# P normalised before it is split, and P times V in four column tiles, for 30 of the 64 attention groups

## The chip, the cores and the metric

One Trainium2 chip, one of its cores. The metric is the device time of the whole kernel in microseconds (us); the time of an execution is that from launch to end on this core.

## What is computed

A cross-attention layer and a gated feed-forward layer, each with a residual, on 16 sequences of 128 tokens and 1024 features.

```python
query, key, value = norm(x) @ w_q.T, ctx @ w_k.T, ctx @ w_v.T      # 32 heads of 32, 8 groups of keys and values
scores    = einsum('bghnd,bgsd->bghns', query, key) / 32 ** 0.5
scores    = where(mask, scores, finfo.min)
attention = softmax(scores)
out       = einsum('bghns,bgsd->bghnd', attention, value)          # P times V
x = x + out @ w_out.T
x12 = norm(x) @ w12.T + b12; x1, x2 = split(x12)
x = x + (silu(x1) * x2) @ w3.T + b3
```

## The kernel before

The tokens are worked through in 8 blocks of two sequences (`U = 2`). A block has 8 groups; group g holds four heads of both sequences, thus 8 score tiles of 128x128. There are 64 groups, and the main loop `for t in range(1, NB + 1): for s in range(STEPS)` runs one step for each: step g = 8(t-1)+s does the scores of group g, and beside them the projections of block t and the output projection of block t-2. The feed-forward layer follows the loop; its first 512 tokens begin in the loop's last block.

Each engine has its own queue, written out by hand in the same order of steps, and no engine changes the order of its queue.

- TensorE in step g: `scores(g)` (8 matmuls, L1406), the step's first unit (`product`, L1349: a projection, or a quarter of an output projection), `turn_attn(g-3)` (two transposes, L1366), the second unit, `weigh(g-2)` (24 matmuls, L1424 to L1428). The last step of a block has the two V projections as its units, four half tiles of the rows of x to transpose (`turn_x`, L1358) around `turn_attn`, and a small transpose and product (`turn_top` L1335, `spread_top` L1342).
- `weigh(g)`: P transposed (128 x 128, two fp16 pieces, high and low) is the stationary operand, V (32 columns and a column of ones) streams. Three products for each of 8 heads; the column of ones gives the row sum of P. The result goes to `B_AV`. VectorE divides it by the row sums (`divide`, L1836 and L1838), TensorE turns it, and ScalarE and VectorE split it into two fp16 pieces (`attn_hi` L1125, `attn_lo` L1844) for the output projection.
- ScalarE in step g: `exps(g, 0)` (four heads, L1153, in place in `e`), the first unit's high piece, `attn_hi(g-3)`, `exps(g, 1)`, the second unit's high piece, `prob_hi(g)` (the high piece of P, L1160), and in steps 4 and 6 `scale_rows` (L1236). In the last step of a block its queue is `exps`, the V projection's high piece (`v_hi`, L1144), two of `x_hi` (L1118), `attn_hi`, `exps`, two of `x_hi`, `v_hi`, `prob_hi`.
- VectorE in step g: `divide(g-3)`, `mask_scores(g)` (8 instructions, L1820), low pieces of the units (L1790), `attn_lo(g-3)`, and maxima, row statistics and residuals as they fall. Up to group 11 it also makes the low piece of P (L1830).
- GpSimd (POOL) in step g: `prob_lo(g-1)` (two instructions, L936) from group 12 on; in the first two steps of a block `split_ctx` (four pieces of three instructions each, L870 to L874); in steps 2 and 3 a `root` (L884, a power of minus one half on one column, and L891).
- The queue of SyncE issues all DMAs, among them `turn_prob(g)` (L699, a transposing DMA of P from `p_split` to `prob_t`) in step g+1, after it has waited for the low piece of P and for `weigh(g-2)`.

`e`, `p_split` and `prob_t` have two buffers each, used by group parity. The results of TensorE's units, transposes of x and turned attention outputs rotate through five PSUM banks (`begin`): a unit waits until VectorE has read what stood in its bank. By that rotation, in the last step of a block the second half of the second x tile takes the bank of the first V projection, and the second V projection that of the first x half.

## Time and profile before

| | us |
|---|---|
| median of 3 runs | 1043.22 |
| lowest, highest | 1041.37, 1044.38 |
| span of the profiled execution, first to last instruction | 1040.4 |
| TensorE busy in it | 1017.7 (98%) |
| VectorE, ScalarE, POOL busy in it | 661.6, 447.3, 498.6 |

The span leaves out what lies around the instructions: 2.8 us against the median. In the views, PE is TensorE's matmuls, PEld its weight loads, DVE is VectorE, ACT ScalarE, POOL GpSimd, SPq the queue of SyncE. A matmul's duration counts its way through the array, so consecutive matmuls overlap in the listing, and what one costs is read from start to start. In a timeline a row can hold several instructions (x24) of one line.

### The profile page before, as it was taken

What the parts mean: (1) busy time and instruction counts of PE and PEld (TensorE: products, weight loads), DVE (VectorE), ACT (ScalarE), POOL (GpSimd) and SP (SyncE); (2) the same over time, 40 slices, a digit from 0 to 9 for tenths busy, and PEclk for the clock granted to TensorE, in tenths of its full rate; (3) what the DMA queues carried; (4) which work ended last, traced back from release to release, by engine and by line L of the source; (5) the groups of instructions that cost most, each with busy time, mean ns of one, the idle gap of its engine ahead of it and who ended that gap; (6) DMA issues with size and microseconds to landing.
All of it is one profiled execution on the core that took longest, in us unless ns stands there. A gap on an engine that the chain in (4) does not pass through costs nothing.

```text
span 1040.4 us, 21876 instructions
## 1 busy us (share of the span) xinstructions
PE 1017.7 (98%) x8400; PEld 695.6 (67%) x8400; DVE 661.6 (64%) x2080; ACT 447.3 (43%) x983; POOL 498.6 (48%) x476
## 2 busy tenths in 40 slices
PE   7897999999999999999999999999999999999998
PEld 6786868869687696886655544444444888468853
DVE  6789977767787777888646234636864447625431
ACT  6768556557465574664766210123431112202100
POOL 2869923727337273379958596158742301212000
PEclk9999999999999999999999999999999999999999
DMA  9669686998989999789946715494758631974201
GB/s 367 227 160 197 168 216 168 222 247 222 248 211 229 230 245 244 179 236 232 268 94 123 253 71 203 94 345 160 272 200 185 235 112 40 236 230 122 83 31 51
DMA packets 230776, 199.12 MB, mean 191 GB/s; under 512 B 177040, under 2 KB 187280, under 8 KB 225808
## 3 DMA queue, kind: packets, MB, share of 16 engines
q1 hardware_dynamic: 230672, 197.72, 69.0%
q8 instruction: 67, 1.10, 0.4%
q14 instruction: 37, 0.30, 0.1%
HBM read 119.04 MB, written 35.65 MB: 149 GB/s over the span
## 4 chain that ended last, share of the span: by engine, by line
PE 87%; DVE 6%; DMA 1%; ACT 1%; issue 0%; SPq 0%; DVEq 0%
PE bank_dense L1349 52%; PE bank_spare L1349 13%; PE bank_score L1494 6%; PE bank_spare L1494 6%; PE bank_av L1494 3%; PE bank_score L1406 2%; DVE arena_attn L1820 2%; DVE arena_attn L1830 1%; PE bank_av L1424 1%; PE bank_av L1428 1%; PE bank_av L1426 1%; PE bank_dense L1366 1%; DMA k_scratch<-arena_in 1%; PE bank_spare L1358 0%; PE bank_dense L1358 0%
## 5 line engine op out<-in xcount | busy, mean ns | idle before, releaser
L1153 ACT ACTIVATE arena_attn<-arena_attn,arena_in 128x128 f32<-128x128 f32 x512 | 162.7, 391 | 94.6 <-DVE arena_in L1820 93.6
L1349 PE MATMUL bank_dense<-arena_rows,arena_in 128*128 128x256 f16 (+1 forms) x1272 | 175.2, 295 | 1.9 <-POOL arena_in L874 1.0
L936 POOL TENSOR_TENSOR arena_attn<-arena_attn 128x512 f16<-128x512 f32 x89 | 102.6, 1170 | 148.8 <-ACT arena_attn L1160 148.8
L1349 PE MATMUL bank_dense<-arena_attn,arena_rows 128*128 128x512 f16 x768 | 166.4, 379 | 0.0
L1349 PEld LDWEIGHTS bank_dense<-arena_rows,arena_in 128*128 128x128 f16 x1272 | 123.0, 98 | 43.1 <-DVE arena_in L1668 1.6
L1820 DVE CUSTOM_DVE_ANT_0 arena_attn<-bank_score,arena_in 128x128 f32<-128x128 f32 x512 | 143.5, 346 | 0.4 <-PE bank_score L1406 0.4
L1349 PEld LDWEIGHTS bank_dense<-arena_attn,arena_rows 128*128 128x128 f16 x768 | 75.2, 98 | 90.2
L1349 PE MATMUL bank_dense<-arena_out,arena_attn 128*128 128x512 f16 x576 | 127.8, 379 | 0.0
L1349 PEld LDWEIGHTS bank_dense<-arena_out,arena_attn 128*128 128x128 f16 x576 | 55.5, 98 | 63.3
L1349 PE MATMUL bank_spare<-arena_rows,arena_in 128*128 128x256 f16 (+1 forms) x648 | 87.6, 292 | 0.0
L1349 PE MATMUL bank_dense<-arena_out,arena_in 128*128 128x512 f16 x384 | 83.0, 379 | 0.0
L874 POOL TENSOR_TENSOR arena_in<-arena_in 128x512 f16<-128x512 f32 x62 | 74.2, 1196 | 5.0
L1349 PEld LDWEIGHTS bank_spare<-arena_rows,arena_in 128*128 128x128 f16 x648 | 63.0, 98 | 19.0
L1907 DVE SCALAR_TENSOR_TENSOR arena_out<-bank_dense,small,arena_out 128x256 f32<-128x256 f32 x64 | 28.0, 478 | 75.0 <-PE bank_dense L1349 75.0
L884 POOL TENSOR_TENSOR small<-small 128x1 f32<-128x1 f32 x32 | 19.9, 622 | 107.2 <-DVE small L1709 107.2
L1349 PEld LDWEIGHTS bank_dense<-arena_out,arena_in 128*128 128x128 f16 x384 | 37.6, 98 | 45.3
L1160 ACT ACTIVATE arena_attn<-arena_attn 128x1024 f16<-128x1024 f32 x64 | 67.2, 1050 | 1.0 <-DMA arena_attn<-arena_attn 0.7
L1349 PE MATMUL bank_dense<-arena_in 128*128 128x256 f16 x456 | 52.8, 273 | 1.4 <-DVE arena_in L1675 1.4
L1424 PE MATMUL bank_av<-v_high,arena_attn 128*128 128x33 f16 x512 | 45.5, 178 | 6.7 <-DMA arena_attn<-arena_attn 6.7
L1003 POOL TENSOR_TENSOR arena_out<-arena_out,arena_rows 128x1024 f32<-128x1024 f32 x12 | 29.2, 2462 | 47.1 <-DMA arena_out<-x_scratch 47.1
L1859 DVE SCALAR_TENSOR_TENSOR arena_rows<-bank_dense,small,arena_rows 128x256 f32<-128x256 f32 x48 | 21.0, 479 | 46.9 <-PE bank_dense L1349 43.9
L1349 PEld LDWEIGHTS bank_dense<-arena_in 128*128 128x128 f16 x456 | 43.8, 98 | 7.8 <-DVE arena_in L1675 1.7
(219 smaller groups left out, 1890.8 us busy)
## 6 DMA issues: line engine op xcount, KB each, us to landing
arena_rows<-x SPq DMA_DIRECT2D x32, 512.0 KB, 6.1
arena_in<-w_scratch SPq DMA_DIRECT2D x64, 256.0 KB, 3.1
arena_attn<-q_scratch SPq DMA_DIRECT2D x48, 256.0 KB, 4.5
arena_rows<-w_t SPq DMA_DIRECT2D x12, 1024.0 KB, 6.2
arena_rows<-ctx_t SPq DMA_DIRECT2D x8, 1024.0 KB, 6.1
q_scratch<-arena_attn SPq DMA_DIRECT2D x16, 512.0 KB, 5.1
x_scratch<-arena_rows SPq DMA_DIRECT2D x16, 512.0 KB, 3.8
arena_out<-x_scratch SPq DMA_DIRECT2D x16, 512.0 KB, 5.9
```

What stands on the lines that cost most here:

```text
L874: pool.tensor_tensor(lo, buf, hi, ALU.subtract).then_inc(ready, 1)
L936: ins = pool.tensor_tensor(p_split[:, g % 2, u, 1], e[:, g % 2, u], p_split[:, g % 2, u, 0], ALU.subtract)
L1003: ins = pool.tensor_tensor(y_res[:, u], y_res[:, u], b3_all, ALU.add)
L1153: ins = act.activation(head, head, ACT.Exp, bias=neg_max[:, g % 2, h:h + 1], scale=-1.0)
L1160: act.activation(p_split[:, g % 2, :, 0], e[:, g % 2], ACT.Copy).then_inc(s_phi, 1)
L1349: ins = pe.matmul(dst, lhs(a, c), rhs(b, c), start=(c == chunks[0] and n == 0), stop=(c == chunks[-1] and n == 2))
L1406: ins = pe.matmul(B_SCORE[:, HALF * u + SEQ * j:HALF * u + SEQ * j + SEQ], q_stack[0:3 * DH, m // 4, j, m % 4, SEQ * u:SEQ * u + SEQ], k_s ...
L1424: pe.matmul(B_AV[:, at:at + VW], prob_t[:, g % 2, u, 0, j], v_high[:, a % 2, u, m], start=True, stop=False)
L1494: ins = pe.matmul(seven(v, j), weights[:, a, P * c:P * c + P], rows[:, b, c], start=(c == 0 and n == 0), stop=(c == 3 and n == 2))
L1820: ins = dve.tensor_tensor_reduce(out=e[:, g % 2, h // HPG, SEQ * (h % HPG):SEQ * (h % HPG) + SEQ], in0=B_SCORE[:, SEQ * h:SEQ * h + SEQ], ...
L1859: ins = dve.scalar_tensor_tensor(out=cols, in0=bank("o", b, q)[:, 256 * n:256 * n + 256], scalar=c_out[:, 2 * h + n:2 * h + n + 1], in1=co ...
L1907: ins = dve.scalar_tensor_tensor(out=cols, in0=bank("y", f, q)[:, 256 * k:256 * k + 256], scalar=c_ffn[:, 2 * h + k:2 * h + k + 1], in1=co ...
```

## The change

For the groups of `NORMED` (from 8 to 47, those with g mod 8 of 2 or more: 30 groups, six in each of five blocks):

- `exps` has each Exp also sum its row (`accum_out`, into `p_sum`).
- GpSimd, in step g behind `prob_lo(g-1)`, runs `norm_prob(g)`: for each half, when its `exps` are done, `p_sum` times 2^-14, to the power -1 (both on 128x4), and P times that (128x512, in place in `e`). `by_vector` holds for no group, so VectorE's `norm_prob` is never called.
- `prob_hi(g)` waits for that instead of for `exps`. The rest of the split of P is as before.
- `weigh(g)` has V's 32 columns as the stationary operand and P transposed (128 columns) as the moving one, 24 matmuls, those of head j in column tile j (`tile_position=(0, 32 j)`). The result is the turned output, written into a rotating bank. There is no `divide` and no `turn_attn`.
- `weigh(g)` stands where `turn_attn(g)` stood, in the middle of step g+3, no longer at the end of step g+2.
- `attn_hi` and `attn_lo` take off the 2^14.
- waits on `s_av` and `s_avread` count only the divided groups, or are for the `a` result (`weighed`).

```diff
+NORMED = [g for g in range(8, 48) if g % 8 >= 2]
+P_SCALE = 2.0 ** 14
...
+        def weighed(g):
+
+            return (s_dense, done("a", g)) if g in NORMED else (s_av, divided_count(g))
...
                 if g >= 2:
-                    sp.wait_ge(s_av, g - 1)
+                    sp.wait_ge(*weighed(g - 2))
                 sp.dma_start_transpose(prob_t[:, g % 2].rearrange("p u s j n -> p (u s j) n"),
...
+            def norm_prob(g):
+                n = normed_count(g - 1, by_pool)
+                for u in range(U):
+                    pool.wait_ge(s_exp, 2 * g + u + 1)
+                    pool.tensor_scalar(inv_pool[:, u], p_sum[:, g % 2, u], 1 / P_SCALE, None, ALU.mult).then_inc(s_pinv, 1)
+                    pool.wait_ge(s_pinv, 2 * (U * n + u) + 1)
+                    pool.tensor_tensor(inv_pool[:, u], inv_pool[:, u], minus_one.broadcast_to([P, HPG]), ALU.pow)\
+                        .then_inc(s_pinv, 1)
+                    pool.wait_ge(s_pinv, 2 * (U * n + u) + 2)
+                    heads = e[:, g % 2, u].rearrange("p (j n) -> p j n", j=HPG)
+                    ins = pool.tensor_tensor(heads, heads, inv_pool[:, u].rearrange("p (j o) -> p j o", o=1)
+                                             .broadcast_to([P, HPG, SEQ]), ALU.mult)
+                ins.then_inc(s_pnorm, 1)
...
                     if GROUPS * (t - 1) + s > PLO_ALONE:
                         prob_lo(GROUPS * (t - 1) + s - 1)
+                    if by_pool(GROUPS * (t - 1) + s):
+                        norm_prob(GROUPS * (t - 1) + s)
                     if t < NB and s in (0, 1):
                         split_ctx(t, halves[s])
...
-                    ins = act.activation(head, head, ACT.Exp, bias=neg_max[:, g % 2, h:h + 1], scale=-1.0)
+                    if g in NORMED:
+                        ins = act.activation(head, head, ACT.Exp, bias=neg_max[:, g % 2, h:h + 1], scale=-1.0,
+                                             accum_out=p_sum[:, g % 2, u, j:j + 1])
...
             def prob_hi(g):
-                act.wait_ge(s_exp, 2 * g + 2)
+                if by_pool(g):
+                    act.wait_ge(s_pnorm, normed_count(g, by_pool))
...
+                if g in NORMED:
+                    dst = begin("a", g)
+                    terms_of_out = ((v_high, 0), (v_low, 0), (v_high, 1))
+                    for u in range(U):
+                        for n, (v, piece) in enumerate(terms_of_out):
+                            for j in range(HPG):
+                                ins = pe.matmul(dst[DH * j:DH * j + DH, SEQ * u:SEQ * u + SEQ],
+                                                v[:, a % 2, u, m, 0:DH], prob_t[:, g % 2, u, piece, j],
+                                                start=n == 0, stop=n == 2, tile_position=(0, DH * j))
+                    ins.then_inc(s_dense, 1)
+                    return
...
-                    if g >= 3:
+                    if g >= 3 and g - 3 in NORMED:
+                        weigh(g - 3)
+                    elif g >= 3:
                         turn_attn(g - 3)
...
-                    if g >= 2:
+                    if g >= 2 and g - 2 not in NORMED:
                         weigh(g - 2)
...
             def divide(g):
+                if g in NORMED:
+                    return
```

## Rows read from the trace of the kernel before

**Rows 1.** The page: busy time of each engine; the chain that ended last, by engine.

```profile
PE 1017.7 (98%) x8400; PEld 695.6 (67%) x8400; DVE 661.6 (64%) x2080; ACT 447.3 (43%) x983; POOL 498.6 (48%) x476
...
PE 87%; DVE 6%; DMA 1%; ACT 1%; issue 0%; SPq 0%; DVEq 0%
```

**Rows 2.** Window, us: length, busy (instructions) of PE, PEld, DVE, ACT, POOL; clock, DMA.

```profile
135.00:200.00 65.00, 65.00 (x678) 50.06 (x677) 47.46 (x205) 38.33 (x98) 28.22 (x32) 1.00 0.80 199
```

**Rows 3.** Timeline of PE (start, duration, engine, line), end of one step.

```profile
211.78 0.38 PE L1366 MATMUL bank_dense<-arena_in 128*128 128x128 f32 x2
211.99 2.78 PE L1349 MATMUL bank_dense<-arena_in 128*128 128x256 f16 x24
214.61 0.18 PE L1424 MATMUL bank_av<-v_high,arena_attn 128*128 128x33 f16 x1
...
215.22 0.61 PE L1406 MATMUL bank_score<-arena_attn 96*128 96x128 f16 x8
215.66 0.60 PE L1349 MATMUL bank_dense<-arena_out,arena_attn 128*128 128x512 f16 x2
```

**Rows 4.** Timeline of PE, last step of a block, and the same of the block before.

```profile
168.69 0.61 PE L1406 MATMUL bank_score<-arena_attn 96*128 96x128 f16 x8
...
233.35 0.61 PE L1406 MATMUL bank_score<-arena_attn 96*128 96x128 f16 x8
233.79 0.27 PE L1335 MATMUL bank_spare<-arena_in 128*1 128x128 f32 x1
233.91 2.78 PE L1349 MATMUL bank_spare<-arena_in 128*128 128x256 f16 x24
...
237.62 1.04 PE L1358 MATMUL bank_spare<-arena_in,arena_rows 128*128 128x128 f32 x8
238.54 0.28 PE L1349 MATMUL bank_dense<-arena_in 128*128 128x256 f16 x1
```

**Rows 5.** Timeline of ACT, step of group 22 and its successor, the last of its block.

```profile
230.33 0.38 ACT L1125 ACTIVATE arena_attn<-bank_dense 128x256 f16<-128x256 f32 x1 [2.52 <-PE bank_dense L1366]
230.61 1.26 ACT L1153 ACTIVATE arena_attn<-arena_attn,arena_in 128x128 f32<-128x128 f32 x4
...
233.23 1.05 ACT L1160 ACTIVATE arena_attn<-arena_attn 128x1024 f16<-128x1024 f32 x1
234.18 1.23 ACT L1236 ACTIVATE arena_rows<-arena_rows,arena_in,small 128x1024 f32<-128x1024 f32 x1
235.53 1.28 ACT L1153 ACTIVATE arena_attn<-arena_attn,arena_in 128x128 f32<-128x128 f32 x4
236.78 0.39 ACT L1144 ACTIVATE v_high<-bank_spare 128x256 f16<-128x256 f32 x1
```

**Rows 6.** Timeline of DVE in the same step.

```profile
237.42 0.41 DVE L1790 SCALAR_TENSOR_TENSOR v_low<-bank_spare,v_high 128x256 f16<-128x256 f32 x1
```

**Rows 7.** Timeline of POOL: a root, prob_lo, and the start of the context's split.

```profile
135.21 0.55 POOL L884 TENSOR_TENSOR small<-small 128x1 f32<-128x1 f32 x1 [4.50 <-DVE small L1709]
135.84 0.19 POOL L891 TENSOR_TENSOR arena_in<-arena_in,small 128x1 f32<-128x1 f32 x1
...
178.12 2.28 POOL L936 TENSOR_TENSOR arena_attn<-arena_attn 128x512 f16<-128x512 f32 x2 [6.15 <-ACT arena_attn L1160]
180.35 1.04 POOL L870 TENSOR_TENSOR arena_in<-arena_rows,small 128x512 f32<-128x512 f32 x1
181.46 0.61 POOL L872 CAST arena_in<-arena_in 128x512 f16<-128x512 f32 x1
...
186.30 2.28 POOL L936 TENSOR_TENSOR arena_attn<-arena_attn 128x512 f16<-128x512 f32 x2
```

**Rows 8.** Timeline of ACT at the start: the read of a row sum and the next activation.

```profile
10.65 0.19 ACT L1031 ACTIVATION_READ_ACCUMULATOR arena_in<-arena_attn 128x1 f32 x1
10.75 1.04 ACT L1031 ACTIVATE arena_in<-arena_attn 128x1024 bf16<-128x1024 f32 x1
```

**Rows 9.** DMA issues: kind, count, median us to landing; transposes of P.

```profile
arena_attn<-arena_attn SPq DMA_TRANSPOSE x64, 4.9
```

More of the change, by code:

```diff
@@ L302, in later_unit, with by_vector, by_pool, normed_count @@
     return UNITS * (f - PLAIN) + i
+def by_vector(g):
+    return g in NORMED and g % GROUPS < 2
+def by_pool(g):
+    return g in NORMED and g % GROUPS >= 2
+def normed_count(g, kind=lambda n: n in NORMED):
+    return sum(kind(n) for n in range(g + 1))
+def divided_count(g):
+    return g + 1 - normed_count(g)
 def plo_count(g):
@@ L409, in xattn_ffn @@
         kept, with_6, with_5, with_7 = [terms[:, 0], terms[:, 1]], terms[:, 2], terms[:, 3], terms[:, 4]
+        p_sum = part(arena_attn, 59, 1, F32)[:, 0:2 * U * HPG].rearrange("p (r u j) -> p r u j", r=2, u=U)
+        inv_pool = part(arena_attn, 60, 1, F32)[:, 0:U * HPG].rearrange("p (u j) -> p u j", u=U)
+        minus_one = part(arena_attn, 62, 1, F32)[:, 0:1]
+        inv_vector = part(arena_attn, 61, 1, F32)[:, 0:U * HPG].rearrange("p (u j) -> p u j", u=U)
         k_stack = part(arena_attn, 63, 4).rearrange("p (b g n) -> p b g n", b=2, g=4)
@@ L1124, in attn_hi @@
                     act.wait_ge(s_dense, done("o", (g - RING) // GROUPS, 3))
-                act.activation(attn_t[:, g % RING, 0], bank("a", g)[:, 0:AB], ACT.Copy).then_inc(s_dhi, 1)
+                act.activation(attn_t[:, g % RING, 0], bank("a", g)[:, 0:AB], ACT.Copy,
+                               scale=1 / P_SCALE if g in NORMED else 1.0).then_inc(s_dhi, 1)
             def q_hi(t, m):
@@ L1362, in turn_attn @@
             def turn_attn(g):
-                pe.wait_ge(s_avread, g + 1)
+                pe.wait_ge(s_avread, divided_count(g))
                 dst = begin("a", g)
@@ L1831, in prob_lo, with norm_prob @@
                    .then_inc(s_plo, 1)
+            def norm_prob(g):
+                n = normed_count(g - 1, by_vector)
+                for u in range(U):
+                    dve.wait_ge(s_exp, 2 * g + u + 1)
+                    dve.reciprocal(inv_vector[:, u], p_sum[:, g % 2, u]).then_inc(s_vinv, 1)
+                    dve.wait_ge(s_vinv, U * n + u + 1)
+                    heads = e[:, g % 2, u].rearrange("p (j n) -> p j n", j=HPG)
+                    ins = dve.scalar_tensor_tensor(out=heads, in0=heads, scalar=P_SCALE,
+                                                   in1=inv_vector[:, u].rearrange("p (j o) -> p j o", o=1)
+                                                   .broadcast_to([P, HPG, SEQ]), op0=ALU.mult, op1=ALU.mult)
+                ins.then_inc(s_vnorm, 1)
             def divide(g):
+                if g in NORMED:
+                    return
                 av = B_AV[:, 0:VW * U * HPG].rearrange("p (h w) -> p h w", w=VW)
-                dve.wait_ge(s_av, g + 1)
+                dve.wait_ge(s_av, divided_count(g))
                 dve.reciprocal(inv_sum[:, :].rearrange("p (h o) -> p h o", o=1), av[:, :, DH:DH + 1]).then_inc(s_inv, 1)
-                dve.wait_ge(s_inv, g + 1)
+                dve.wait_ge(s_inv, divided_count(g))
                 dve.tensor_tensor(attn.rearrange("p (h w) -> p h w", w=DH), av[:, :, 0:DH],
@@ L1843, in attn_lo @@
                 dve.wait_ge(s_dhi, hi_count("a", g))
+                if g in NORMED:
+                    dve.scalar_tensor_tensor(out=attn_t[:, g % RING, 1], in0=bank("a", g)[:, 0:AB], scalar=1 / P_SCALE,
+                                             in1=attn_t[:, g % RING, 0], op0=ALU.mult, op1=ALU.subtract).then_inc(s_dread, 1)
+                    return
                 dve.tensor_tensor(attn_t[:, g % RING, 1], bank("a", g)[:, 0:AB], attn_t[:, g % RING, 0], ALU.subtract)\
@@ L2007, in _ @@
                         attn_lo(g - 3)
+                    if by_vector(g):
+                        norm_prob(g)
                     if t < NB - 1 and s == 5:
```

23 lines of the change are left out of this document (17 added, 6 removed).

## The prediction

> **What bounds the kernel now.** I read the page first: TensorE is busy for 98% of the span and carries 87% of the chain that ended last; no other engine is above 64% [rows 1]. A busy share alone doesn't say that TensorE sets the pace, so I took windows over the main loop: from 135 to 200 us TensorE is busy for all 65.00 us at full clock, VectorE for 47.46, ScalarE for 38.33 and GpSimd for 28.22 [rows 2]. All of the changed groups but the first few run in such windows, from about 125 to 460 us. So a microsecond taken from TensorE there is a microsecond of the kernel, as long as the other queues keep up. The reader should see in the timelines how near they are to not keeping up. A block of the loop takes 233.35 - 168.69 = 64.66 us [rows 4], and the five changed blocks repeat it.
>
> **TensorE's part.** Removed per group: two transposes, 211.99 - 211.78 = 0.21 us from start to start, and 24 matmuls of 33 columns, 215.22 - 214.61 = 0.61 us, which is 25 ns each [rows 3]. Together 0.82 us. Added: 24 matmuls whose moving operand has 128 columns and whose stationary one has 32. No row shows a column tile at work beside another. The bounds come from two rows. If the tiles don't overlap, each costs what a 128-column score matmul costs: eight in 215.66 - 215.22 = 0.44 us [rows 3], 55 ns each, 24 in 1.32 us. If four overlap fully, six rounds of 55 ns make 0.33 us. I take 0.60 us, since a matmul with its own weight load has never been issued here faster than 25 ns [rows 3] and four tiles in turn at that pace leave each tile 100 ns for its 55. Gain 0.22 us per group, over 30 groups 6.6 us; bounds: a gain of 0.49 x 30 = 14.7 us, a loss of 0.50 x 30 = 15 us.
>
> A switch of the array's tiling might cost something too. The transpose of one column of maxima (L1335) is the only instruction in this stretch that isn't a full-width one. It starts with the last score matmul of the eight still in flight (233.35 + 0.61 = 233.96) and the next product starts 0.12 us after it, against 0.11 for a transpose in the full array [rows 3, 4]. I cost the switch at 0.01 us at most. The Trainium skill ("TensorEngine Tiling (Array Packing)", Tiling Modes) says that a change of tiling mode drains the engine. By that rule each changed group would pay twice; the row doesn't show it.
>
> **ScalarE's and GpSimd's part.** Added on ScalarE: eight reads of a row sum. Such a read delays the next activation by 10.75 - 10.65 = 0.10 us [rows 8]: 0.8 us per group, 0.4 for each half. Bounds: zero, and 0.19 each, the read's own duration. Added on GpSimd, per half: a small multiply (0.19 and a handover of 0.08), a power on 4 columns, and a 128x512 multiply with fp32 out. Rows: a power on one column takes 0.55 us, 0.63 until its dependant starts; the same kind of 128x512 multiply 181.46 - 180.35 = 1.11 us [rows 7]. With the power at 0.63 that is 0.27 + 0.63 + 1.11 = 2.0 us, and with something for three more columns 2.1 us. Call this n. The upper bound takes all that a power costs above a plain one-column instruction, 0.55 - 0.19 = 0.36 us, once per column: n = 2.0 + 3 x 0.36 = 3.1 us. I take 2.1, because both other small instructions here are mostly fixed cost, and keep 3.1 as the end.
>
> What hides this? GpSimd has the time on average, but the work sits between `exps` and `prob_hi`, and ScalarE's queue waits there. Behind `prob_hi(g)` stand `scale_rows`, `exps(g+1, 0)`, the unit's high piece and `attn_hi`, and behind those VectorE's low pieces, which free TensorE's banks. I walked the tightest place, the last step of a block, on the trace's own clock:
> - The new P times V of group 19 ends at 229.91 + 0.60 = 230.51 instead of 230.13 for the turn, so `exps(22, 1)` starts 0.39 later than its 230.61, at 231.0 [rows 5]. It takes four Exps of 0.30 and four reads of 0.10, ends at 232.7, and GpSimd's second half ends at 232.7 + 2.1 = 234.8.
> - `prob_hi(22)` starts then instead of at 233.23: 1.6 us late. `scale_rows` follows, and `exps(23, 0)` is 1.6 late and 0.4 longer, so `v_hi` starts near 236.78 + 2.0 = 238.8 [rows 5]. VectorE's low piece, which ended at 237.42 + 0.41 = 237.83 [rows 6], now ends near 239.6.
> - TensorE's second half of the second x tile takes that bank. It started at 237.62 + 0.46 = 238.08 [rows 4]: a slack of only 0.25 us. In the new order it comes at about 238.25 (0.22 sooner from the step before, 0.39 later for the product in the middle). It waits 1.1 to 1.4 us, and the second V projection some 0.3 us more for the next bank.
> So about 1.5 us per block, in five blocks 7.5 us, go to a wait that isn't in the trace of before. (229.91 and 230.13 are the starts of the turn and the next product there; from 230.33 of [rows 5] and a latency of 0.4 they follow.) In the other steps I find slack: `attn_hi` and the units' high pieces come 1 to 1.5 us later, and five banks cover that.
>
> Whether GpSimd itself becomes the bound: its loop through a block is three `prob_lo` of 2.28, the context's split of 186.30 - 180.35 = 5.95 us twice [rows 7], two roots of 0.8 and 12n, and in six places a `prob_hi` of 1.05 plus two handovers of 0.1 for which it waits, and five more `prob_lo`. That is 18.2 + 11.9 + 1.6 + 12n + 7.5 = 39.2 + 12n. At n = 2.1 it is 64.4 us, against TensorE's 64.66 - 1.3 + 1.5 = 64.9. They are as good as level: above n = 2.1 each tenth more costs about 1.2 us per block.
>
> **What costs nothing.** VectorE loses a division and a reciprocal per changed group and gains nothing; it isn't the bound. `turn_prob(g)` now waits for the product in the middle of step g+1, not the end of step g, and the stores, loads and spills behind it on SyncE's queue go later by up to 4 us. A transpose lands 4.9 us after issue [rows 9] and is wanted two steps, thus 13 us or more, later; `stack_q` and `stack_k` are issued two steps or more ahead. If that cover were gone, TensorE would wait for the transpose before the product. The earliest changed groups, 10 and 11, still have VectorE's `prob_lo` behind a later `prob_hi`; ScalarE has 3 us of idle time there. The constant written at the start falls into GpSimd's first wait.
>
> **Sum.** 6.6 us saved, 7.5 us lost in five last steps, and some 0.5 us for the level GpSimd loop: 1.4 us longer. Against the profiled execution 1040.4 + 1.4 = 1041.8; what lies around it is 2.8 us by the median, so 1044.6, said as 1045. About 0.3% (3.1 us) is what a measurement can tell from no change.
>
> **The rivals.**
> - *The power costs by the column.* GpSimd's loop becomes the bound. At n = 2.5 the block takes 39.2 + 30 = 69.2 us, 4.5 more than before: five blocks 22 us, 1066. At n = 3.1 it takes 76.4, 59 us in all, 1102. It decides from n = 2.1 on. For it: an excess of 0.36 us for a single column is much if it were all fixed. Against: GpSimd is idle for more than half of the window [rows 2]. Its likeliest size is near 1062. Chance 0.27.
> - *The stall is smaller and the tiles overlap better.* If the row sum's read hides, ScalarE is 0.8 us earlier and the stall halves: -6.6 + 3.5 = -3. If also the tiles run nearer to 0.33 us, up to 8 us are added (GpSimd allowing): 1033 to 1040, likeliest 1037. For it: rows of P streaming in four tiles have 100 ns each for 55. Against: the read's 0.10 is shown. Chance 0.25.
> - *The tiles don't overlap.* The change doesn't do what it is built on. 15 us more on TensorE, the stall mostly stays: 1043.2 + 15 + 4 = 1062. Chance 0.05.
> - *Each switch of tiling drains the array.* A matmul of 256 columns takes 0.28 us of which 0.11 is its turn [rows 4], so 0.17 us twice for 30 groups, 10 us: 1055. Chance 0.05. The Trainium skill's sentence on the drain (same page and section) would make this come true.
> - *The forecast.* Chance 0.38, 1041 to 1048.
>
> **Chances.** Faster by over 0.3% (under 1040.1): the second rival and a little of the forecast, 0.27. Slower by over 0.3% (over 1046.3): the first, third and fourth, less a little, and the forecast's upper edge, 0.40. Within: 0.33. Both signs hold much, so the forecast's own range is 1041 to 1048; the range for 8 in 10 takes in most of the second rival and the power up to n = 2.5: 1035 to 1066.
>
> **What would show it.** 24 starts of the new product within 0.60 us; no gap around it. A wait of TensorE at L1358 in the last step of each block, put down to VectorE's low piece of V, 1.1 to 1.4 us, and one before the second V projection. GpSimd's power on 128x4 near 0.6 us and its 128x512 multiply near 1.1. A wait of `prob_hi` for GpSimd of 1 to 2 us. The prediction is wrong if the power takes over 1 us, if the product takes 1.3 us, or if TensorE shows no wait at L1358.

## The result, and the profile after

The changed kernel takes 1061.77 us (median of 4 runs, 1061.37 to 1062.79) against 1043.72 for the kernel before on the same chip (4 runs): a ratio of 1.0171, 95% interval 1.0143 to 1.0198. It is slower. The span of its profiled execution is 1060.0 us, 19.6 more than before.

Line numbers of the changed kernel in the views: L1411 is a product of a unit, L1468 scores, L1489 the new P times V, L1497 the old one, L1420 `turn_x`, L1207 and L1210 the Exps with and without a row sum, L1222 `prob_hi`, L1298 `scale_rows`, L1197 `v_hi`, L1865 the low piece of a unit, L1731 VectorE's search for a maximum of a weight tile (the "look"), L972 `prob_lo`, and L979, L981, L985 the three instructions of `norm_prob`: small multiply, power, large multiply.

The page of the changed kernel, busy time of each engine and the chain that ended last, by engine:

```profile
PE 1021.2 (96%) x8340; PEld 684.8 (65%) x8340; DVE 652.4 (62%) x2020; ACT 465.2 (44%) x1223; POOL 638.0 (60%) x657
...
PE 58%; POOL 20%; ACT 6%; DVE 5%; issue 4%; DMA 2%; SPq 0%; DVEq 0%; POOLq 0%
```

TensorE carried 87% of the chain before [rows 1] and carries 58% now; GpSimd has 20%, where it had no entry. The same stretch as [rows 2] and the next one (length, busy time of PE, PEld, DVE, ACT, POOL, then granted clock, DMA):

```profile
135.00:200.00 65.00, 63.30 (x656) 46.52 (x655) 43.17 (x183) 42.25 (x146) 52.75 (x63) 0.97 0.75 189
200.00:265.00 65.00, 60.97 (x609) 44.07 (x607) 42.70 (x182) 39.46 (x137) 54.42 (x65) 0.97 0.86 214
```

GpSimd went from 28.22 to 52.75 busy in 65, and TensorE is no longer always at work. But a busy share of 0.84 (54.42 of 65 in the second window) isn't a full engine. Most of what is left of GpSimd's time is waiting in a ring with ScalarE: GpSimd's low piece of P needs ScalarE's high piece, that one needs GpSimd's normalisation, and this stands behind the low piece in GpSimd's queue. Its timeline from the step before the last of a block into the last (start, duration, engine, line):

```profile
231.40 2.27 POOL L972 TENSOR_TENSOR arena_attn<-arena_attn 128x512 f16<-128x512 f32 x2 [1.17 <-ACT arena_attn L1222]
233.75 0.23 POOL L979 TENSOR_SCALAR arena_attn<-arena_attn 128x4 f32<-128x4 f32 x1
234.06 1.04 POOL L981 TENSOR_TENSOR arena_attn<-arena_attn 128x4 f32<-128x4 f32 x1
235.17 1.04 POOL L985 TENSOR_TENSOR arena_attn<-arena_attn 128x512 f32<-128x512 f32 x1
236.28 0.23 POOL L979 TENSOR_SCALAR arena_attn<-arena_attn 128x4 f32<-128x4 f32 x1
...
237.71 1.04 POOL L985 TENSOR_TENSOR arena_attn<-arena_attn 128x512 f32<-128x512 f32 x1
239.91 2.27 POOL L972 TENSOR_TENSOR arena_attn<-arena_attn 128x512 f16<-128x512 f32 x2 [1.17 <-ACT arena_attn L1222]
```

One half of `norm_prob` takes 236.28 - 233.75 = 2.53 us. The power on 128x4 takes as long as a multiply on 128x512. The ring is `prob_lo(g-1)` 2.35, the two halves 2.53 and 2.46, and a wait of 1.17 for `prob_hi(g)`: 239.91 - 231.40 = 8.51 us for a step. The long steps (8.46 to 9.07 us) can hold that. The short ones at the start of a block (6.25 us), where GpSimd also splits the context, can't, so `prob_hi` gets late at once and stays late: in this block it starts 6.7 us after the first score of its step in the first two steps, 12.4 in the third and 13.6 to 14.1 in the four behind it, where before it was 9.0 us in these four. The delay is paid at the end of the block. There ScalarE waits:

```profile
234.57 0.36 ACT L1184 ACTIVATE arena_attn<-bank_dense 128x256 f16<-128x256 f32 x1
238.78 1.06 ACT L1222 ACTIVATE arena_attn<-arena_attn 128x1024 f16<-128x1024 f32 x1 [3.85 <-POOL arena_attn L985]
239.74 1.23 ACT L1298 ACTIVATE arena_rows<-arena_rows,arena_in,small 128x1024 f32<-128x1024 f32 x1
...
242.41 0.36 ACT L1197 ACTIVATE v_high<-bank_spare 128x256 f16<-128x256 f32 x1
```

And TensorE waits behind it, in the last step of the block (timeline of PE):

```profile
233.94 0.61 PE L1468 MATMUL bank_score<-arena_attn 96*128 96x128 f16 x8
...
241.02 0.66 PE L1420 MATMUL bank_spare<-arena_in,arena_rows 128*128 128x128 f32 x4 [2.42 <-ACT arena_rows L1298]
243.29 1.12 PE L1420 MATMUL bank_spare<-arena_in,arena_rows 128*128 128x128 f32 x4 [1.61 <-DVE v_low L1865]
244.19 4.03 PE L1411 MATMUL bank_dense<-arena_in 128*128 128x256 f16 x24
248.15 0.38 PE L1404 MATMUL bank_dense<-small,arena_in 1*128 1x2 f32 x2
248.46 0.62 PE L1468 MATMUL bank_score<-arena_attn 96*128 96x128 f16 x8
```

The step takes 248.46 - 233.94 = 14.52 us, against 8.84 in the same block before. Three parts can be read, which make 5.3 of these 5.7 us: 2.42 us until the rows that ScalarE scales are there, 1.61 us until the first V projection's bank is free, and 4.03 us for a unit that takes 2.78 elsewhere [rows 3]. The last is the clock. Windows of this kernel after the wait (columns as above, clock third from the end):

```profile
243.00:244.00 1.00, 0.71 (x4) 0.71 (x4) 0.95 (x3) 1.00 (x4) 0.94 (x1) 0.66 0.57 115
244.00:245.00 1.00, 1.00 (x6) 0.71 (x5) 0.90 (x2) 1.00 (x6) 0.98 (x1) 0.50 1.16 216
245.00:246.00 1.00, 1.00 (x7) 0.70 (x5) 0.00 (x0) 1.00 (x6) 0.35 (x3) 0.50 1.19 249
```

After the two waits the granted clock falls from 1.00 to 0.50 (1.2 GHz) and returns to 1.00 at 247 us. In the five last steps the wait for the scaled rows is nothing, 2.42, 2.82, 2.42 and 1.62 us, the one for the bank 1.61 in each, and from the unit's first start to the next instruction's it is 4.39, 3.96, 5.03, 4.20 and 3.74 us, where it takes 2.71 at full clock.

Read from scores to scores, the loss sits in five steps. The last steps of the five changed blocks take 12.38, 14.52, 16.06, 14.61 and 13.51 us, 71.1 together, against 8.85, 8.84, 8.85, 8.84 and 9.18, together 44.6: 26.5 us more. The other 35 steps of these blocks take 274.6 us against 280.9: 6.3 us less. The rest of the kernel is within 0.7 us of before.

The first of the five blocks shows that a GpSimd which is behind with its work isn't needed for the loss. It has only four low pieces of P to make there instead of eight (they begin at group 12), and it stands still for the Exps on the way (timeline of POOL):

```profile
139.22 0.23 POOL L979 TENSOR_SCALAR arena_attn<-arena_attn 128x4 f32<-128x4 f32 x1 [1.94 <-ACT arena_attn L1207]
155.96 0.23 POOL L979 TENSOR_SCALAR arena_attn<-arena_attn 128x4 f32<-128x4 f32 x1 [0.40 <-ACT arena_attn L1207]
```

Still its seventh `prob_hi` starts 11.2 us after the step's first score, against 8.95 before, and its last step takes 12.38 us. What TensorE feels is how late `prob_hi` is in its step; a full loop of GpSimd is one way to make it late, the length of the normalisation itself is another.

### The profile page after: what moved, and what is told of

Read it like the earlier page. It is cut to its first block, busy times and chain, and to the rows that moved or that the text cites. A ratio compares the mean times of both kernels' runs of the same rounds, so it can differ in the third digit from the quotient of the medians.

```text
span 1060.0 us, 22087 instructions
## 1 busy us (share of the span) xinstructions
PE 1021.2 (96%) x8340; PEld 684.8 (65%) x8340; DVE 652.4 (62%) x2020; ACT 465.2 (44%) x1223; POOL 638.0 (60%) x657
## 3 DMA queue, kind: packets, MB, share of 16 engines
q1 hardware_dynamic: 230672, 197.72, 69.1%
## 4 chain that ended last, share of the span: by engine, by line
PE 58%; POOL 20%; ACT 6%; DVE 5%; issue 4%; DMA 2%; SPq 0%; DVEq 0%; POOLq 0%
PE bank_dense L1411 36%; PE bank_score L1567 6%; PE bank_spare L1567 5%; PE bank_spare L1411 5%; POOL arena_attn L981 5%; POOL arena_attn L985 5%; POOL arena_attn L972 5%; PE bank_av L1567 3%; ACT arena_attn L1207 2%; ACT arena_attn L1222 2%; DVE arena_attn L1895 2%; POOL arena_in L908 2%; POOL arena_in L904 2%; POOL arena_attn L979 1%; DVE arena_attn L1905 1%
## 5 line engine op out<-in xcount | busy, mean ns | idle before, releaser
L1411 PE MATMUL bank_dense<-arena_rows,arena_in 128*128 128x256 f16 (+1 forms) x1272 | 175.5, 295 | 1.7 <-POOL arena_in L908 1.0
L1411 PE MATMUL bank_dense<-arena_attn,arena_rows 128*128 128x512 f16 x768 | 166.4, 379 | 0.0
L1411 PEld LDWEIGHTS bank_dense<-arena_rows,arena_in 128*128 128x128 f16 x1272 | 121.7, 98 | 44.6 <-DVE arena_in L1743 1.4
L1411 PEld LDWEIGHTS bank_dense<-arena_attn,arena_rows 128*128 128x128 f16 x768 | 75.2, 98 | 90.2
L972 POOL TENSOR_TENSOR arena_attn<-arena_attn 128x512 f16<-128x512 f32 x89 | 103.3, 1178 | 44.0 <-ACT arena_attn L1222 44.0
L1411 PE MATMUL bank_dense<-arena_out,arena_attn 128*128 128x512 f16 x576 | 127.8, 379 | 0.0
L1222 ACT ACTIVATE arena_attn<-arena_attn 128x1024 f16<-128x1024 f32 x64 | 67.4, 1053 | 92.9 <-POOL arena_attn L985 92.5
L1210 ACT ACTIVATE arena_attn<-arena_attn,arena_in 128x128 f32<-128x128 f32 x272 | 86.3, 391 | 49.3 <-DVE arena_in L1895 49.0
L1411 PEld LDWEIGHTS bank_dense<-arena_out,arena_attn 128*128 128x128 f16 x576 | 55.4, 98 | 63.5
L1207 ACT ACTIVATE arena_attn<-arena_attn,arena_in 128x128 f32<-128x128 f32 x240 | 92.6, 389 | 6.1 <-DVE arena_in L1895 6.1
L1411 PE MATMUL bank_spare<-arena_rows,arena_in 128*128 128x256 f16 (+1 forms) x648 | 87.7, 292 | 0.0
L1411 PE MATMUL bank_dense<-arena_out,arena_in 128*128 128x512 f16 x384 | 83.0, 379 | 0.0
L1411 PEld LDWEIGHTS bank_spare<-arena_rows,arena_in 128*128 128x128 f16 x648 | 62.3, 98 | 19.8
L1411 PEld LDWEIGHTS bank_dense<-arena_out,arena_in 128*128 128x128 f16 x384 | 37.6, 98 | 45.3
L985 POOL TENSOR_TENSOR arena_attn<-arena_attn 128x512 f32<-128x512 f32 x60 | 62.4, 1039 | 4.7
L981 POOL TENSOR_TENSOR arena_attn<-arena_attn 128x4 f32<-128x4 f32 x60 | 62.1, 1035 | 5.0
L1411 PE MATMUL bank_dense<-arena_in 128*128 128x256 f16 x456 | 60.5, 296 | 1.5 <-DVE arena_in L1750 1.4
```

What stands on the lines that cost most here:

```text
L972: ins = pool.tensor_tensor(p_split[:, g % 2, u, 1], e[:, g % 2, u], p_split[:, g % 2, u, 0], ALU.subtract)
L981: pool.tensor_tensor(inv_pool[:, u], inv_pool[:, u], minus_one.broadcast_to([P, HPG]), ALU.pow)\
L985: ins = pool.tensor_tensor(heads, heads, inv_pool[:, u].rearrange("p (j o) -> p j o", o=1) .broadcast_to([P, HPG, SEQ]), ALU.mult)
L1207: ins = act.activation(head, head, ACT.Exp, bias=neg_max[:, g % 2, h:h + 1], scale=-1.0, accum_out=p_sum[:, g % 2, u, j:j + 1])
L1210: ins = act.activation(head, head, ACT.Exp, bias=neg_max[:, g % 2, h:h + 1], scale=-1.0)
L1222: act.activation(p_split[:, g % 2, :, 0], e[:, g % 2], ACT.Copy).then_inc(s_phi, 1)
```

## The experiments

"Last steps" is the sum of the last steps of the five changed blocks and "five blocks" their whole length, from start to start of the scores in the profiled execution. Ratios stand against the kernel before on the same chip.

| kernel | ratio, 95% interval | last steps | five blocks |
|---|---|---|---|
| before | 1 | 44.6 | 325.5 |
| after | 1.0171 (1.0143 to 1.0198) | 71.1 | 345.7 |
| no power | 0.9954 (0.9938 to 0.9971) | 45.8 | 319.4 |
| no normalisation | 0.9920 (0.9902 to 0.9938) | 42.8 | 320.4 |
| row sums alone | 0.9958 (0.9942 to 0.9975) | 44.7 | 318.1 |
| transposes in the wait | 1.0145 (1.0124 to 1.0166) | 65.4 | 341.0 |
| look first | 1.0202 (1.0175 to 1.0229) | 71.8 | 345.0 |
| four groups | 0.9999 (0.9985 to 1.0014) | 49.4 | 325.1 |
| four groups, look first | 1.0005 (0.9989 to 1.0021) | 45.1 | 322.2 |
| four groups, two looks first | 1.0001 (0.9983 to 1.0019) | 47.3 | 324.5 |
| without the seventh group | 1.0069 (1.0054 to 1.0084) | 55.4 | 331.2 |
| inverse on VectorE | 1.0267 (1.0251 to 1.0282) | 69.9 | 350.9 |
| the same, look first | 1.0080 (1.0066 to 1.0094) | 59.5 | 333.0 |

**The power left out.** P is multiplied by its scaled row sum instead of the inverse, so the output differs.

```diff
-                    pool.tensor_tensor(inv_pool[:, u], inv_pool[:, u], minus_one.broadcast_to([P, HPG]), ALU.pow)
```

> The changed kernel without GpSimd's power on the row sums (P is multiplied by its scaled row sum instead of by the inverse; the output differs for that reason). GpSimd's part per half falls from 2.54 to about 1.43 us. Theory (the loop of GpSimd's normalisation and ScalarE's high piece of P is the bound, and the power's cost by the column carries it over TensorE's pace): the five last steps fall from 12.4 to 16.1 us to about 9.3, and the time to about 1041 us (1039 to 1044). Rival (the ScalarE reads of the row sums, or the tiled product, cost the time): it stays above 1055 us.

Measured: 1037.77 us against 1042.93. The last steps fall from 71.1 to 45.8 us, each of them 9.16 or 9.17, the other steps stay as in the changed kernel. GpSimd's half is now this (timeline; L982 is the large multiply):

```profile
230.76 0.22 POOL L979 TENSOR_SCALAR arena_attn<-arena_attn 128x4 f32<-128x4 f32 x1 [2.60 <-ACT arena_attn L1204]
231.06 1.04 POOL L982 TENSOR_TENSOR arena_attn<-arena_attn 128x512 f32<-128x512 f32 x1
```

It takes 231.06 + 1.04 - 230.76 = 1.34 us. From 135 to 460 us GpSimd now waits 54.8 us for the Exps (9.4 in the changed kernel) and ScalarE's `prob_hi` 22.9 us for GpSimd (92.5); the seventh `prob_hi` starts 9.7 us after the step's first score. So 25.3 of the 26.5 us hang on one instruction of 1.04 us, sixty times.

**No sums and no normalisation.** The output isn't divided by the row sums.

```diff
-                    if by_pool(GROUPS * (t - 1) + s):
-                        norm_prob(GROUPS * (t - 1) + s)
...
-                                             accum_out=p_sum[:, g % 2, u, j:j + 1])
```

> The tiled product and its place alone: no row sums, no normalisation (the output isn't divided by the row sums), the high piece of P waits for the exponentials as before. Theory: TensorE gains 0.26 us per changed group and nothing else moves: 30 x 0.26 = 7.8 us, 1036 us (1034 to 1038). Rival (the tiled product with its switches of tiling, or its later place, costs elsewhere): 1041 us or more.

Measured: 1034.84 us against 1042.93, 0.8% less. This is what the product in column tiles is worth by itself. In blocks 2, 3 and 5 a block takes 63.05 to 63.98 us, against 64.65 in the undisturbed blocks before, and 63.05 is the clean one: 1.6 us for six groups, 0.27 each, 8.0 us for thirty. Block 4 has 3.7 us more than the others in its third and fourth steps (TensorE waits 2.3 us for a transposing DMA there); the changed kernel shows nothing of the sort in its five blocks.

**Row sums alone.** The Exps sum their rows, GpSimd does nothing with it; not divided either.

> As the one without normalisation, but with the row sums read by ScalarE in the 30 groups (0.8 us each; output not divided). Theory: ScalarE has room for them in all but the last step of a block, 1038 us (1036 to 1040). Rival (the reads are what delays ScalarE): above 1045 us.

Measured: 1038.10 us against 1042.93, last steps of 8.76 us (one of 9.64) against 8.55 to 8.56 without the sums. The read of the sum costs 0.2 us in the last step and nothing in the others. Its own price in ScalarE's queue is as forecast (timeline of the changed kernel):

```profile
231.22 0.39 ACT L1207 ACTIVATE arena_attn<-arena_attn,arena_in 128x128 f32<-128x128 f32 x1
231.52 0.18 ACT L1207 ACTIVATION_READ_ACCUMULATOR arena_attn<-arena_attn,arena_in 128x1 f32 x1
231.61 0.38 ACT L1207 ACTIVATE arena_attn<-arena_attn,arena_in 128x128 f32<-128x128 f32 x1
```

Exps start 0.39 us apart where they took 1.26 / 4 = 0.31 [rows 5]. The three kernels give a sum for the last steps: 42.8 with the product alone, 1.9 for the sums (0.9 of it in one step), 1.1 more for everything of the normalisation except the power, 25.3 for the power.

**Transposes in the wait.** The changed kernel, with 28 idle transposes behind the product of the last step, so that TensorE doesn't stand still.

```diff
+                        if g - 3 in NORMED:
+                            for _ in range(28):
+                                pe.transpose(B_AV[:, 0:P], ident[:, :], ident[:, :])
```

> The changed kernel with 28 transposes of the identity into the unused bank in each changed last step, 3.1 us of work in the place where TensorE waits 2.4 us. Theory: a part of the loss is the lower clock after the waits (the V projection there took 4.0 us instead of 2.8): with the wait filled the clock stays at full, last steps get 1.2 us shorter, 1056 us (1053 to 1059). Rival (the clock costs nothing, since ScalarE is behind anyway): 1061 us or more.

Measured: 1058.06 us against 1042.67, ratio 1.0145. The granted clock in windows of 65 us is 1.00 where it was 0.95 to 0.97, and the last steps get 5.7 us shorter. The unit behind the waits takes 2.71 or 2.72 us in each of them, 13.6 in all, against 21.3 in the changed kernel: 7.7 us is what the low clock costs that unit. The 5.7 us are less, since the transposes take 3.1 us themselves, more than the wait that they fill in any block: in the first block TensorE has no wait left in the last step, and it still takes 11.60 us. In the other four the wait for VectorE's low piece is still there, 1.00 to 1.61 us. Over the whole kernel the gain is smaller again: 4.7 us in the five blocks, and by the two ratios (1.0171 and 1.0145) 2.7 us.

**The order of the products.** On the kernel without normalisation: the three products of one head in a row in one column tile, in place of four heads in turn.

```diff
-                        for n, (v, piece) in enumerate(terms_of_out):
-                            for j in range(HPG):
+                        for j in range(HPG):
+                            for n, (v, piece) in enumerate(terms_of_out):
```

> The variant without normalisation, with the three products of a head issued one behind the other in the same column tile, not four tiles in turn. Theory (four tiles overlap only when issued in turn): 24 matmuls take about 1.0 us instead of 0.37, each changed step 0.6 us longer, 1035 + 18 = 1053 us. Rival (order doesn't matter): as the variant without normalisation, 1035 us.

Measured: 1035.02 us in one run; the steps with the new product are 0.01 to 0.02 us longer. My theory of matmuls that need another tile to overlap with fell: in a row in one tile they are as fast. The timeline of PE shows how:

```profile
228.25 0.26 PE L1481 MATMUL bank_dense<-arena_attn,v_high 128*32 128x128 f16 x4
228.32 0.25 PE L1481 MATMUL bank_dense<-arena_attn,v_low 128*32 128x128 f16 x4
```

The program has v_high, v_low, v_high for one head and then for the next. The trace has the first products of four heads start together and their second ones 0.07 us later: the four tiles work side by side here too.

**Four groups of eight.** The third to the sixth of each block. It computes the reference.

```diff
-NORMED = [g for g in range(8, 48) if g % 8 >= 2]
+NORMED = [g for g in range(8, 48) if 2 <= g % 8 <= 5]
```

> The changed kernel with only the third to sixth group of each block (20 groups) taken the new way. Theory: in the seventh and eighth step neither ScalarE nor GpSimd waits for a normalisation, so the last step of a block is as before (8.8 us), and 20 x 0.26 = 5.2 us are gained less some tenths: 1039 us (1038 to 1042). Rival (the loss is spread over all changed steps): two thirds of the loss remain, 1055 us.

Measured: 1043.43 us against 1042.93, no gain. The four groups win their quarter of a microsecond each, but the first step of a block grows from 6.51 to 6.86 (it holds a new product and an old one), and the last steps still take 49.4 us. What is late there is not GpSimd: the seventh `prob_hi` of each block starts 9.29 us after the step's first score, as without any normalisation. And the first of the five blocks, the only one in which no weight tile is looked at, takes 8.55 us in its last step, the other four 9.41 to 11.34. Waits of VectorE from 135 to 460 us (us in total, times, longest):

```profile
DVE arena_in L1731 <- DMA arena_rows<-w_t: 15.6, 8, 3.3
```

The kernel before has 0.5 us of this wait in that stretch. The DMA queue's timeline:

```profile
221.85 2.69 SPq L733 DMA_TRANSPOSE arena_attn<-arena_attn  x1
225.05 0.36 SPq L757 DMA_DIRECT2D arena_rows<-w_t  x1
```

The load of the weight tile that VectorE looks through stands behind the transposing DMA in SyncE's queue, and that now goes later. VectorE stands still for it in the last step, and TensorE waits for what VectorE does after it (timeline of PE; L1693 follows the look in VectorE's queue):

```profile
237.48 0.63 PE L1420 MATMUL bank_spare<-arena_in,arena_rows 128*128 128x128 f32 x4 [1.06 <-DVE small L1693]
```

**The look loads first.** Tried on the changed kernel and on the one with four groups: the loads go ahead of the transposing DMA.

```diff
+                    if 3 <= t < 7 and s == 5:
+                        load_look(look_at(t, 6), w12_t[2 * (t - 3) + 1])
                     if g >= 1:
                         turn_prob(g - 1)
...
-                    if 3 <= t < 7 and s == 5:
-                        load_look(look_at(t, 6), w12_t[2 * (t - 3) + 1])
```

(and the same for the loads of steps 0 and 3)

> The changed kernel (six groups) with the same loads ahead of the transpose. Theory: with six groups ScalarE waits for GpSimd 5.6 us ahead of the last step and that covers VectorE's wait: 1059 us (1056 to 1062), last steps still over 12 us. Rival (the late load is a cost of its own that adds up): 1052 us or less.

> Third to sixth group of each block the new way, and SyncE's queue issues the weights that are only looked at for their maximum ahead of the transpose of P instead of behind it. Theory (the last step's 9.4 to 11.3 us with four groups came from VectorE waiting for that load, 2 to 3 us late behind the transpose): last steps at 8.6 us, the gain of 20 x 0.26 = 5.2 us shows, 1038 us (1036.5 to 1040). Rival (ScalarE's late high piece does it): no change, 1043 us.

Measured: 1063.95 us with six groups, no help. With four groups 1044.78 us against 1042.67 by the medians, 1043.92 against 1043.33 by the means, which isn't the gain that I expected. Inside the blocks it works: VectorE's wait for the load falls from 15.6 to 2.4 us, the last steps to 45.1 us, the five blocks to 322.2. The load of step 0 however pushes back the transposing DMA for an old product (second steps of 6.70 to 7.16 us in four of the blocks, 6.52 before). In this profiled execution the kernel's start, up to the first changed block, also took 118.2 us, against 111.7 before and 111.0 to 113.5 in the others. So I left the load of step 0 where it was:

> A kernel that computes the reference: four of eight groups per block divided by their row sums (third to sixth), and of the three look loads per block those of steps 3 and 5 ahead of the transposing DMA on SyncE's queue, that of step 0 behind it, where it stood. Theory: with four groups GpSimd's backlog is worked off before the last step; what is left of the loss are late look loads (1 and 4 us of the last steps) and, where all three loads went first, transposing DMAs that came late for the second product of a block (steps of 7.16 us in place of 6.53, in two of five blocks, some 2 us in all). Then the last steps are about 8.6 to 9.4 us as with all three first, the second steps 6.5, and blocks 1 to 5 take about 320 us against 325.5 before: some 1038 us in all, ratio 0.995. Rival: what the last step loses comes from the load of step 0 too, or start-up (block 0) takes what is won: the ratio is 0.999 to 1.001 as with all three first.

Measured: 1043.11 us against 1043.64, last steps of 8.55, 10.25, 9.23, 8.91 and 10.37. The second steps are back at 6.52, and the last steps have lost what that brings. Missed again. The profiled executions take 3.3 and 1.0 us less in the five blocks than before, the medians show neither; single runs of these kernels and of before scatter over 6 to 8 us, so I leave open whether there is a gain of that size.

**Without the seventh group.** Five groups, of which the one just before the last step isn't normalised.

> Five groups of each block: the third to sixth and the eighth, not the seventh, whose normalisation ScalarE waits for right ahead of the last step. Theory A (place: the wait in front of the last step does most of the harm): most of the loss goes, last steps at 9 to 10.5 us, 1043 us (1040 to 1047). Theory B (amount: GpSimd's loop of 39.2 us plus 12 n is simply too long): 5 of 6 groups still leave last steps of 12 us, 1055 us.

Measured: 1049.14 us against 1042.29, between the two theories. Last steps of 8.76, 10.53, 12.64, 10.34 and 13.13. GpSimd enters them without a backlog (it waits for ScalarE 1.79 us before the half at 236.60), yet VectorE waits 15.6 us for look loads in all, as with four groups. In the first block, where no weight tile is looked at, the last step takes 8.76 us, as with the row sums alone. In the other four the seventh `prob_hi` starts 9.3 to 9.7 us after the step's first score, near the 9.29 of the kernel without normalisation, and TensorE waits 0.85 to 1.84 us for L1693, which follows the look in VectorE's queue, then 0.41 us for the low piece of V. So the loss comes by VectorE's queue, in the blocks with looks. How it divides between the late loads and pieces that ScalarE delivers late to VectorE (1.44 us at 230.11) isn't measured.

**The inverse on VectorE.** A reciprocal and a multiply on 128x4 on VectorE in place of power and small multiply on GpSimd, all six groups; then with the look loads first as well.

```diff
+            def invert(g, u):
+                dve.wait_ge(s_exp, 2 * g + u + 1)
...
+                dve.reciprocal(inv_vector[:, u], p_sum[:, g % 2, u]).then_inc(s_vinv, 1)
+                dve.wait_ge(s_vinv, U * normed_count(g - 1) + u + 1)
+                dve.tensor_scalar(inv_pool[:, u], inv_vector[:, u], P_SCALE, None, ALU.mult).then_inc(s_pinv, 1)
```

> The same without moving the loads. Theory: VectorE waits for the late loads again, 2 to 4 us more in some last steps: 1042 us (1038 to 1047), slower than with the loads ahead by 2 to 6 us. Rival (the loads don't matter, as with six groups and the power on GpSimd): equal to the one with the loads ahead.

> All six groups; VectorE makes the scaled inverse of the row sums (a reciprocal and a multiply on 128x4 per half, behind the low pieces of the first and second unit), GpSimd only multiplies P by it, and the loads for the maxima go ahead of the transpose of P. Theory: GpSimd's part falls from 2.54 to about 1.15 us per half, but the second half's inverse waits for VectorE's low piece of the second unit; last steps near 9 to 10 us, 1038 us (1035 to 1043), at or under the kernel before. Rival (any wait of ScalarE for a normalisation costs the last step as much): above 1050 us.

Measured: 1070.74 us and 1051.03 us against 1042.29. Both are slower than before. The two instructions cost 0.17 and 0.20 us, but they stand in VectorE's queue, and GpSimd waits for them (a wait that contains the Exps' own time). Waits of POOL from 135 to 460 us in the first of the two:

```profile
POOL arena_attn L980 <- DVE arena_attn L1921: 104.0, 50, 4.5
```

The order of the loads, worth nothing where GpSimd was last, is worth 20 us here, where VectorE with its look loads stands in the ring: without it, VectorE waits 10.0 us for these loads and TensorE 5.4 us for late transposing DMAs in that stretch. With the look first this remains in a last step (first the timeline of PE, then that of DVE; L1415 is `turn_x`, L1293 `scale_rows`, L1860 the low piece):

```profile
238.38 0.65 PE L1415 MATMUL bank_spare<-arena_in,arena_rows 128*128 128x128 f32 x4 [0.16 <-ACT arena_rows L1293]
240.65 0.66 PE L1415 MATMUL bank_spare<-arena_in,arena_rows 128*128 128x128 f32 x4 [1.61 <-DVE v_low L1860]
```

```profile
240.17 0.42 DVE L1860 SCALAR_TENSOR_TENSOR v_low<-bank_spare,v_high 128x256 f16<-128x256 f32 x1 [1.72 <-ACT v_high L1192]
```

The 1.61 us are the same as in the changed kernel at 243.29. As soon as `scale_rows` is what releases TensorE, the second wait is fixed: behind `scale_rows` ScalarE has four Exps (1.54 us) before `v_hi`, then comes VectorE's low piece, while TensorE has only four transposes to do. So the last step has a cliff, which a late `prob_hi` triggers once it uses up the slack of `scale_rows`. Its height shows in the second and third block of this kernel: 10.87 us where the step takes 8.55 without normalisation, at full clock. In the other three the unit behind the waits takes 4.20 to 4.39 us for 2.72, and the steps 12.25 to 12.94. GpSimd is busy for 42.76 of 65 us here (200 to 265 us), so this isn't a full engine either: the seventh `prob_hi` starts 11.3 to 11.8 us after the step's first score.

No kernel that computes the reference was faster than the kernel before by more than the measurement can tell.

## Why the prediction was right or wrong

I forecast 1045 us in a range of 1035 to 1066. The time is 1061.8: inside the range, on the side that I had given 0.40, and not in the forecast's own 1041 to 1048. One of my own signs of being wrong came true as well: the power takes over 1 us. What came true is the rival "the power costs by the column", with "likeliest near 1062".

- *TensorE's part: right in size, by two errors that nearly cancel.* A gain of 0.22 us per group was forecast, 0.26 to 0.27 measured: steps of 6.25 us for 6.51, a slot of 0.82 - 0.26 = 0.56 us where I had 0.60. I took 25 ns as the least distance of two matmuls and 0.01 us for the switch of tiling. The timeline of PE in the changed kernel (222.118 to 222.6 us) shows the product between a 512-column unit and a 256-column one:

```profile
221.74 0.38 PE L1411 MATMUL bank_dense<-arena_out,arena_attn 128*128 128x512 f16 x1
222.05 0.24 PE L1489 MATMUL bank_spare<-arena_attn,v_high 128*32 128x128 f16 x4
222.12 0.23 PE L1489 MATMUL bank_spare<-arena_attn,v_low 128*32 128x128 f16 x4
222.17 0.28 PE L1489 MATMUL bank_spare<-arena_attn,v_high 128*32 128x128 f16 x8
222.28 0.23 PE L1489 MATMUL bank_spare<-arena_attn,v_low 128*32 128x128 f16 x4
222.34 0.23 PE L1489 MATMUL bank_spare<-arena_attn,v_high 128*32 128x128 f16 x4
222.50 0.28 PE L1411 MATMUL bank_spare<-arena_rows,arena_in 128*128 128x256 f16 x1
```

The 24 matmuls are six rounds of four, one in each tile, 0.056 us apart after the first. That is my bound "four overlap fully", 0.34 us, and not 0.60. The switches are not free: the first round starts 0.31 us after the last 512-column product, whose turn is 0.22 us (two of them take 0.60 and one 0.38 [rows 3]), and the unit starts 0.16 us after the last round, whose turn is 0.06. Together that is about 0.2 us per group where I had 0.01.
- *The power: the failed step.* I took 0.63 us with little for three more columns, n = 2.1. The row shows 1.04 us, 1.12 until the next start, and n = 2.53. One column takes 0.55 [rows 7], so three more cost 0.49, 0.16 each. Without the power 25.3 of the last steps' 26.5 us are gone. My argument for the low value, that other small instructions are mostly fixed cost, came from instructions without a power in them. The upper bound of 0.36 per column held.
- *GpSimd's loop: near the result, in part by luck.* With n = 2.53 the formula 39.2 + 12n makes 69.6 us per block; the blocks take 68.2, 69.0, 70.6, 69.1 and 68.8. But the formula has eight low pieces of P in a block and the first block only four, GpSimd waits for the Exps in it, and it loses its 3.5 us in the last step all the same. And with five groups, by the same formula some 63 us and so no bound, the blocks take 64.1 to 68.7. What the sum should have asked is how late `prob_hi` is in its step, not only whether GpSimd's work fits into the block. The forecast's other half, that n = 2.1 is about level with TensorE, agrees with n = 1.34 (no power) being free, but no run stood at 2.1.
- *The stall in the last step: right in place, wrong in size.* The wait for VectorE's low piece of V is there in each block, 1.61 us against 1.1 to 1.4. I had only that one, 1.5 us a block. Measured are 5.3 us a block (26.5 / 5). Missing were the wait for `scale_rows` ahead of it (9.3 us in the five blocks), which a later `prob_hi` brings, and the low clock afterwards (7.7 us in five units). In the block shown `prob_hi` starts 4.84 us after the first score of the last step (238.78 - 233.94), where before it started 0.12 us ahead of it [rows 4, 5]: 5.0 us later, and the forecast had 1.6.
- *ScalarE's read of the row sum: right.* 0.08 to 0.10 us each; the kernel with the sums alone shows 0.2 us in the last step.
- *The DMA queue: wrong.* I said that what stands behind `turn_prob` goes up to 4 us later and costs nothing. I had gone through stacks, spills and transposes, and not through the look load: VectorE waits 15.0 us for it in the changed kernel and 0.5 before. With six groups and the power on GpSimd the order of the loads changes nothing; with four groups it takes the last steps from 49.4 to 45.1 us.
- *Each switch drains the array: a price, but a smaller one.* The rival had 2 x 0.17 us per group and 10 us in all. The rows show some 0.2 us per group, 6 us in all, which the faster product more than pays for.
- *The chances.* The rival with the power had a spread of 1062 to 1102 and only its lowest part came true, 0.27 was fair for it. The forecast's 0.38 rested on one choice between 2.0 and 3.1, made by the wrong neighbour.

## What to carry to other kernels

An engine idle for half of the time is not free for work that stands in another engine's queue: what decides is the length of the ring through both (here 8.5 us in steps of 6.3 to 9), how late it makes the piece that others wait for, and where that delay is paid. When the price of an operation is known at one size only and the loop is level at the low end of its bounds, take the excess over a plain instruction as growing with size until a row shows otherwise. And of a queue entry that moves, list every later entry with its consumer; the one that is left out is the one that stalls.

## What was not expected of the hardware

- GpSimd's power on 128x4 takes 1.04 us, on 128x1 0.55: nearly as much for 512 numbers as a multiply for 65536 (1.04).
- Matmuls of 128 moving columns in four column tiles run side by side at full speed. The single starts in the trace are 3 ns apart in a round of four (222.049, 222.052, 222.055, 222.059 us), and the rounds 56 ns apart, what one such matmul takes in the full array (55 ns) [rows 3]. On average that is a start every 14 ns, each with its own weight load. The Trainium skill ("TensorE: Matmul & The Clock Gate", Wait — 56ns, not 53.3ns?) says that the distance of two starts never falls below some 25 ns; that section is on matmuls one behind the other in the whole array, where the 33-column ones here bear it out (25 ns), and for column tiles these rows decide. It says as well (same page, The mechanism) that weight loads overlap matmuls in flight only where the row groups differ. Here all tiles span the same rows, and the weights of the second round load while the first is in flight (timeline of PEld; the first round starts at 222.05 and takes 0.24 us):

```profile
222.06 0.11 PEld L1489 LDWEIGHTS bank_spare<-arena_attn,v_low 128*32 128x32 f16 x4
```

- Ahead of the change of tiling the weight loads pause. In the groups of lines of the changed kernel from 135 to 460 us the pause stands in the last column, as "issue" (27 groups of the new P times V in this stretch):

```profile
L1489 PEld LDWEIGHTS bank_spare<-arena_attn,v_high 128*32 128x32 f16 x224 | 4.8, 96 | 4.0 <-issue 4.0
L1489 PEld LDWEIGHTS bank_dense<-arena_attn,v_high 128*32 128x32 f16 x208 | 4.5, 96 | 3.7 <-issue 3.7
```

That is 7.7 / 27 = 0.29 us of idle weight loading per group, and 0.56 - 6 x 0.056 = 0.22 us of TensorE's time for both switches together. The Trainium skill ("TensorEngine Tiling (Array Packing)", Key Properties) says that a change of mode drains the engine. The time seen here is two thirds of the two times 0.17 us that I had worked out for a full drain, and by the profile's ends the first tiles start (222.05) before the last 512-column product has ended (221.74 + 0.38 = 222.12): a switch costs time, but a full drain isn't shown.
- The same waits don't always lower the clock. In the first of the changed kernel's blocks the one wait of 1.61 us is enough for a unit of 4.39 us in place of 2.71. In the kernel with the inverse on VectorE and the look first, waits of 0.15 or 0.16 and 1.61 us are followed by 2.72 us in two blocks and by 4.39 in a third.
